# Block-turned probabilities placed by DMA, and a values product that runs one unit later

## The chip, the cores and the metric

One core of one Trainium2 chip runs the whole program. The metric is the device time of one execution in microseconds (us). TensorE is PE in the rows of the profile, VectorE DVE, ScalarE ACT, GpSimd POOL, and SyncE SP.

## What is computed

Eight batch elements of 128 rows and 512 columns go through three adapter layers (a base product plus a low-rank product, a product with a selected weight, a low-rank product, each added to its input), and then through an attention layer. There the kernel makes, per batch element and group of four query heads (8 key heads x 8 elements = 64 units):

```python
q = rope(rmsnorm(x @ Wq)); k = rope(rmsnorm(x @ Wk)); v = x @ Wv
k_all, v_all = concat(cached 512 rows, 128 new rows)      # 640 keys, heads of 128
scores = einsum('bqhd,bkhd->bhqk', q, k_all) * SCALE      # masked by cache length
out = softmax(scores) @ v_all, then @ Wo, added to x
```

All of it is f32 in and out. A product that has to be exact is made of three products of rounded parts: hi x hi, hi x lo and lo x hi, where hi is the operand rounded to fp32r and lo the rest.

## The kernel before

Instructions are written out by hand for each engine, in order, with semaphores between them; nothing reorders them. The adapter layers take the first 119 us. Then comes a loop over 64 units; unit n is batch element n & 7 of key head n >> 3.

TensorE's `step(n)` (L870) holds: scores of heads 0 and 1 (`score_pair`, L831, 12 products into three PSUM banks), eight of the twelve products of the next unit's queries (L800), scores of heads 2 and 3, the other four query products, the output product of the unit before (`put_out`, L848, 12 products of 512 columns), the transposes of chunks 0 and 1 of the probabilities (`turn_probs`, L856), the next unit's new key and value (`project_new_key`, L810), and then, chunk by chunk, four transposes of 128x128 and three products of 512 columns (`values`, L862). Among them lie the five transposes of the next unit's rotated queries and key (`turn_rotated`, L823) and the four of the cached keys of the unit after it (`turn_cached`, L816). Turned probabilities and turned keys go through two PSUM banks, `ps_ring`.

The probabilities are made in place: `lowest` (VectorE, L1110: scores from PSUM plus mask, with their minimum), `exps` (ScalarE, L620), `inverse` (VectorE, L1116), `normalize` (ScalarE, L625). Each turned chunk of 128 keys x 512 is evicted twice: rounded by ScalarE (`chunk_high`, L629, `pt_hi`), and its rest by VectorE (`chunk_low`, L1125, `pt_lo`). The values are split in the same way: `values_high` on VectorE (L1080), their rest on GpSimd (L476), the new value's parts on ScalarE and VectorE.

GpSimd (`step`, L468) also makes the rest of the weights, sums the rotated queries, takes the power for the norms (`norm_factors`, L464) and issues the two gathers of cached rows. SP (L331) issues the load of the next input `x_s` once `kv_proj` says that the last one is used, the load of a chunk of weights, and towards the end the stores of the output.

Names that the change and the prediction's steps touch: `kc_lo_out` counts the units whose cached keys are split, `qt_lo_out` those whose rotated queries are, `prob_done` the finished probability heads, `pv_done` the values products, `ot_lo_out` the split outputs, `vn_out` (new) the copies of the new value.

Of the kernel before, what the change touches and what calls it, by code (L numbers as in the profile page):

```python
# [31 lines left out]
AHEAD = B + 1  # L32
THETA = 10000.0
# [13 lines left out]
def build(nc, x, x_t, ids0, ids1, ids2, table, lens, w0_t, bias0, lora_a, lora_b, w1_t, w2_b, w2_a,  # L47
          w_qkvo, q_norm, k_norm, k_rows, v_rows, inv_freq, row_in_table, ident_in, out):
    ctx = ExitStack()
    with ctx:  # L50
# [142 lines left out]
        with ExitStack() as p2:  # L193

            rot_a = sb("rot_a", [P, GROUP + 1, D], scope=p2)
# [13 lines left out]
            v_hi = sb("v_hi", [P, CH, D], F32R, scope=p2)  # L209
            v_lo = sb("v_lo", [P, CH, D], F32R, scope=p2)  # L210
            prob = sb("prob", [P, GROUP, KEYS], scope=p2)
            pt_hi = sb("pt_hi", [P, CH, GROUP * P], F32R, scope=p2)
            pt_lo = sb("pt_lo", [P, CH, GROUP * P], F32R, scope=p2)
            ot_hi = sb("ot_hi", [P, GROUP * P], F32R, scope=p2)
            ot_lo = sb("ot_lo", [P, GROUP * P], F32R, scope=p2)
            mask = sb("mask", [P, KEYS], scope=p2)
# [5 lines left out]
            ps_ring = pb("ps_ring", [P, 2, 512], p2)  # L222
            ps_q = pb("ps_q", [P, 512], p2)
            ps_kv = pb("ps_kv", [P, 512], p2)
            ps_o = pb("ps_o", [P, 512], p2)
# [12 lines left out]
            v_hi_out, v_split, vn_hi_out, vn_lo_out = (psem(s) for s in ("v_round", "v_split", "vn_hi_out", "vn_lo_out"))  # L238
            scores, low_done, exp_done, inv_done, prob_done = (psem(s) for s in ("scores", "low_done", "exp_done", "inv_done", "prob_done"))
            p_turned, pt_hi_out, pt_lo_out = psem("p_turned"), psem("pt_hi_out"), psem("pt_lo_out")  # L240
# [9 lines left out]
            def keys_of(kt, u, lo, hi):  # L250

                return kt[:, bass.ds((u & 1) * KEYS + lo, hi - lo)]

# [3 lines left out]
            with nc.Block() as block:  # L257
                @block.sync
                def _(sp):
# [71 lines left out]
                    def step(n, weights, last, finished):  # L331
                        if not last:
                            sp.wait_ge(kv_proj, n + 1)
                            sp.nop(nofuse=True)
                            sp.dma_start(x_s[:, :, :].bitcast(F32), xt_dram[bass.ds((n + 1) & 7, 1), :, :, :].rearrange("a p s c -> p (a s) c")).then_inc(x_s_in, 16)
                        if weights:
                            sp.wait_ge(w_split, n + AHEAD)
                            sp.dma_start(w_raw[:, 0, :], w_qkvo[bass.ds(n + AHEAD, 1), :, :].rearrange("a p c -> p (a c)")).then_inc(w_raw_in, 16)
                        if finished:
                            sp.wait_ge(y_added, n)  # L340
                            sp.nop(nofuse=True)
                            sp.dma_start(out[bass.ds((n - 1) & 7, 1), :, :].rearrange("a p c -> p (a c)"),
                                         y[:, bass.ds((n - 1) & 7, 1), :].rearrange("p a c -> p (a c)")).then_inc(out_in, 16)
# [921 lines left out]
```

## Time and profile before

| | us |
|---|---|
| median of 3 runs | 1242.81 (1242.17 to 1243.01) |
| profiled execution | 1239.95 |
| its span, first to last instruction | 1238.1 |
| mean granted TensorE clock | 0.993 |

| engine | busy us | share of the span |
|---|---|---|
| PE matmul | 1212.0 | 98% |
| PE weight load | 1038.2 | 84% |
| DVE | 918.8 | 74% |
| ACT | 853.2 | 69% |
| POOL | 545.5 | 44% |

The difference between the span and the execution's time, 1.85 us, lies outside of the instructions. In a timeline row the first number is the start and the second the time from there to the end of the last instruction of the row, so that the start of the next row less that of this one is what the row costs its engine where nothing waits. Brackets at the end of a row give the idle time ahead of it and what ended it. DMA engines are busy for about a quarter of the time.

### The profile page before, as it was taken

How to read it: one execution, taken by the hardware profiler on the slowest of the kernel's cores; microseconds unless marked ns; L12 is line 12 of the kernel's file. 1: busy time of each engine (PE TensorE's matmuls, PEld its weight loads, DVE VectorE, ACT ScalarE, POOL GpSimd, SP SyncE). 2: the span in 40 equal slices, each digit the busy share in tenths (PEclk: the TensorE clock that was granted, in tenths of full speed). 3: DMA queues.
4: the chain of work that ended last, by engine and by line, in shares of the span. 5: the costliest groups of instructions: out<-in, count | busy, mean ns of one | idle time of the engine just before them, and what ended most of it. 6: DMA issues, size and time to landing. Idle time of an engine off the chain costs nothing.

```text
span 1238.1 us, 28992 instructions
## 1 busy us (share of the span) xinstructions
PE 1212.0 (98%) x7072; PEld 1038.2 (84%) x7072; DVE 918.8 (74%) x2295; ACT 853.2 (69%) x2170; POOL 545.5 (44%) x570
## 2 busy tenths in 40 slices
PE   7998999999999999999999999999999999999997
PEld 4565888888888888888888888888888888888885
DVE  2336778777778777787787877877778777777774
ACT  2233777777777777777777777777777777767774
POOL 7761444445444444444444444444544445333430
PEclk9998999999999999999999999999999999999999
DMA  6673222222222222222122222222222222112210
GB/s 193 232 255 107 78 67 78 89 89 67 75 80 89 89 62 80 80 89 89 61 74 87 89 86 65 72 89 89 78 67 77 89 89 69 63 59 85 85 52 25
DMA packets 37607, 109.50 MB, mean 88 GB/s; under 512 B 7512, under 2 KB 7640, under 8 KB 36570
## 3 DMA queue, kind: packets, MB, share of 16 engines
q1 hardware_dynamic: 25288, 68.44, 16.1%
q0 software_dynamic: 11152, 36.72, 10.4%
q10 hardware_dynamic: 1154, 4.19, 0.9%
q8 instruction: 6, 0.10, 0.0%
q14 instruction: 7, 0.06, 0.0%
HBM read 103.03 MB, written 6.29 MB: 88 GB/s over the span
## 4 chain that ended last, share of the span: by engine, by line
PE 96%; DVE 1%; ACT 1%; DMA 1%; issue 1%; POOL 0%; SPq 0%; DVEq 0%; ACTq 0%; POOLq 0%
PE ps_q L794 14%; PE ps_ring L858 12%; PE ps_o L694 11%; PE ps_o L696 11%; PE ps_o L695 11%; PE ps_kv L794 7%; PE ps_s L696 6%; PE ps_s L694 6%; PE ps_s L695 6%; PE ps_l L726 2%; PE ps_ring L820 2%; PE ps_q L828 2%; PE ps_t L688 1%; PE ps_l L742 1%; PE ps_h L712 1%
## 5 line engine op out<-in xcount | busy, mean ns | idle before, releaser
L622 ACT ACTIVATE prob<-prob,low 128x640 f32<-128x640 f32 x256 | 210.8, 824 | 129.0 <-DVE low L1112 128.9
L1028 DVE TENSOR_TENSOR pt_lo<-ps_ring,pt_hi 128x512 fp32r<-128x512 f32 x320 | 209.1, 686 | 87.8 <-ACT pt_hi L582 87.5
L1112 DVE CUSTOM_DVE_ANT_0 prob<-ps_s,mask,q_gain 128x640 f32<-128x640 f32 x256 | 216.3, 882 | 36.8 <-PE ps_s L696 35.0
L103 POOL TENSOR_TENSOR w_lo<-w_raw,w_hi 128x640 f32 (+1 forms) x64 | 100.2, 1565 | 263.6 <-DVE w_hi L97 262.3
L582 ACT ACTIVATE pt_hi<-ps_ring 128x512 fp32r<-128x512 f32 x320 | 181.5, 593 | 33.1 <-PE ps_ring L858 33.0
L627 ACT ACTIVATE prob<-prob,inv 128x640 f32<-128x640 f32 x256 | 196.9, 818 | 0.0
L858 PE MATMUL ps_ring<-ident,prob 128*128 128x128 f32 x1280 | 186.3, 276 | 5.1 <-DVE pt_lo L1028 2.7
L858 PEld LDWEIGHTS ps_ring<-ident,prob 128*128 128x128 f32 x1280 | 149.0, 141 | 40.3 <-DVE pt_lo L1028 9.9
L794 PE MATMUL ps_q<-w_hi,x_s 128*128 (+1 forms) x512 | 171.8, 396 | 0.0
L694 PE MATMUL ps_s<-kt_hi,qt_hi 128*128 (+1 forms) x512 | 159.4, 311 | 1.5 <-DVE low L1112 1.5
L696 PE MATMUL ps_s<-kt_hi,qt_lo 128*128 (+1 forms) x512 | 159.5, 311 | 0.0
L695 PE MATMUL ps_s<-kt_lo,qt_hi 128*128 (+1 forms) x512 | 159.1, 311 | 0.0
L476 POOL TENSOR_TENSOR v_lo<-v_raw,v_hi 128x512 fp32r<-128x512 f32 x64 | 83.4, 1302 | 154.6 <-DVE v_hi L1085 154.6
L694 PE MATMUL ps_o<-pt_hi,v_hi 128*128 128x512 f32 x320 | 147.6, 461 | 0.0
L696 PE MATMUL ps_o<-pt_hi,v_lo 128*128 128x512 f32 x320 | 126.9, 397 | 0.0
L695 PE MATMUL ps_o<-pt_lo,v_hi 128*128 128x512 f32 x320 | 125.6, 392 | 0.0
L466 POOL TENSOR_TENSOR rstd<-var,neg_half 128x5 f32<-128x5 f32 x64 | 77.4, 1209 | 85.9 <-DVE var L1061 85.8
L794 PEld LDWEIGHTS ps_q<-w_hi,x_s 128*128 128x128 f32 x512 | 95.6, 188 | 15.0
L794 PE MATMUL ps_kv<-w_hi,x_s 128*128 (+1 forms) x512 | 106.8, 293 | 0.0
L694 PEld LDWEIGHTS ps_s<-kt_hi,qt_hi 128*128 128x128 f32 x512 | 97.0, 189 | 7.5 <-DVE low L1112 1.8
L694 PE MATMUL ps_o<-w_hi,ot_hi 128*128 (+1 forms) x256 | 101.0, 394 | 1.4 <-DVE ot_lo L1028 1.4
L695 PEld LDWEIGHTS ps_s<-kt_lo,qt_hi 128*128 128x128 f32 x512 | 96.9, 189 | 5.7
(141 smaller groups left out, 2587.8 us busy)
## 6 DMA issues: line engine op xcount, KB each, us to landing
x_s<-xt_split SPq DMA_DIRECT2D x64, 512.0 KB, 3.3
w_raw<-w_qkvo_dram SPq DMA_DIRECT2D x55, 320.0 KB, 3.5
w<-w_t_dram SPq DMA_DIRECT2D x8, 1024.0 KB, 6.8
xt_split<-x3t ACTq DMA_DIRECT2D x8, 512.0 KB, 4.3
w_raw<-w_qkvo_dram POOLq DMA_DIRECT2D x9, 320.0 KB, 4.9
xbt<-x_t_dram SPq DMA_DIRECT2D x8, 256.0 KB, 2.9
xb<-x_dram SPq DMA_DIRECT2D x8, 256.0 KB, 3.7
out_dram<-y SPq DMA_DIRECT2D x8, 256.0 KB, 2.2
```

What stands on the lines that cost most here:

```text
L103: return nc.gpsimd.tensor_tensor(lo, raw, hi.bitcast(F32), ALU.subtract)
L476: nc.gpsimd.tensor_tensor(vl, v_raw[:, :], vh.bitcast(F32), ALU.subtract).then_inc(v_split, 1)
L582: return nc.scalar.activation(dst, src, ACT.Copy)
L622: nc.scalar.activation(prob[:, h, :], prob[:, h, :], ACT.Exp, bias=low[:, h:h + 1], scale=-1.0, accum_out=total[:, h:h + 1]).then_inc(exp_ ...
L627: nc.scalar.activation(prob[:, h, :], prob[:, h, :], ACT.Copy, scale=inv[:, h:h + 1]).then_inc(prob_done, 1)
L694: nc.tensor.matmul(dst, lh, rh, start=first, stop=False)
L695: nc.tensor.matmul(dst, lh, rl, start=False, stop=False)
L696: return nc.tensor.matmul(dst, ll, rh, start=False, stop=final)
L794: mm = nc.tensor.matmul(dst, x_s[:, int(i % 3 == 2), k * P:(k + 1) * P], w_rest if i % 3 == 1 else w, start=i == 0, stop=i == 3 * KT - 1)
L858: mm = nc.tensor.transpose(ps_ring[:, bank, h * P:(h + 1) * P], prob[:, h, c * P:(c + 1) * P], ident[:, :])
L1028: return nc.vector.tensor_tensor(dst, src, high.bitcast(F32), ALU.subtract)
L1112: nc.vector.tensor_tensor_reduce(out=prob[:, h, :], in0=ps_s[:, score_slot(h):score_slot(h) + KEYS], in1=mask[:, :], scale=q_gain[:, h:h + ...
```

## The change

- The probabilities are no longer transposed on TensorE and not split. VectorE transposes each head's 128x640 probabilities in blocks of 32x32 (`turn_blocks`) into `blocks`, and 16 DMAs (`place_block`), each of 32 partitions x 640 f32 (80 KB), put block rows where a full transpose has them, in one of two homes of `prob_t`. SP issues 12 of them, ScalarE 4, after the fourth head's transpose and after the values product of two units before.
- The values product takes `v_raw` and the new value as they are, in plain f32: ten products of 128x128 by 256 columns, in two halves (heads 0, 1 and heads 2, 3) with a PSUM bank each. It stands last in TensorE's `step(n + 1)`. Its second half uses the bank in which the next unit's cached keys have been turned, and waits for `kc_lo_out`.
- The output product and the addition to `y` are made one unit later still (`put_out(n - 2)` in step n).
- The query projection is in one piece between the score pairs. The new key's projection stands right behind the second score pair, the cached keys' transposes behind that, now for unit n + 1.
- ScalarE does the squares of unit n + 1 and the copy of its new value ahead of `exps(n, 2)`. VectorE's order is new as below. GpSimd moves the new value, and issues the gather of values at the start of its step.
- Two more steps are written out in front of the loops, and the end has `put_out` and `values` behind the last step.

```diff
+            def place_block(issuer, n, a, j):
+                issuer.dma_start(prob_t[j * BLOCK:(j + 1) * BLOCK, bass.ds((n & 1) * NB * RUN + a * RUN, RUN)],
+                                 blocks[a * BLOCK:(a + 1) * BLOCK, j, :, :, :].rearrange("p c h q -> p (c h q)")).then_inc(pt_in[j], 16)
...
+                    def place_blocks(n, first=False):      # SP; ScalarE's has a = 3 alone
+                        sp.wait_ge(blocks_turned, GROUP * (n + 1))
+                        if not first:
+                            sp.wait_ge(pv_done, 2 * (n - 1))
+                        for a in range(NB - 1):
+                            for j in range(NB):
+                                place_block(sp, n, a, j)
...
+                    def step(n, last, head=True, out=True, first=False):      # ScalarE
+                        if head:
+                            out_high(n - 2, 1, first=first)
                         exps(n, 0)
                         exps(n, 1)
                         normalize(n, 0)
                         normalize(n, 1)
+                        if not last:
+                            query_squares(n + 1, range(GROUP))
+                            key_squares(n + 1)
+                            new_value(n + 1, first=not out)
                         exps(n, 2)
                         exps(n, 3)
                         normalize(n, 2)
+                        if not last:
+                            scale_key(n + 1)
+                            cached_high(n + 1, ps_o1, first=not out)
                         normalize(n, 3)
                         if not last:
                             rotated_high(n + 1)
+                        if out:
+                            out_high(n - 1, 0, first=not head)
+                        place_blocks(n, first=not head)
...
+                    def values(u, cached, first=False):      # TensorE
+                        pe.wait_ge(v_in, 16 * (u + 1))
+                        pe.wait_ge(vn_moved, u + 1)
+                        for j in range(NB):
+                            pe.wait_ge(pt_in[j], 16 * NB * (u + 1))
+                        if not first:
+                            pe.wait_ge(ot_lo_out, 2 * u)
+                        for pair in (0, 1):
+                            if pair == 1:
+                                pe.wait_ge(kc_lo_out, cached)
+                            for c in range(CH):
+                                v = v_raw[:, c * D:(c + 1) * D] if c < CCH else v_new[:, :]
+                                mm = nc.tensor.matmul(ps_o[pair][:, 0:PAIR], v, turned_probs(u, c, pair),
+                                                      start=c == 0, stop=c == CH - 1)
+                            mm.then_inc(pv_done, 1)
...
+                    def step(n, last, out=True, pv=True, first=False):      # TensorE
                         score_pair(n, 0)
                         if not last:
                             project_queries(n + 1)
                         score_pair(n, 1)
                         if not last:
                             project_new_key(n + 1)
+                            turn_cached(n + 1, ps_o1, 2 * (n - 1) if out else None)
+                        if out:
+                            put_out(n - 2, first=first)
                         if not last:
                             turn_rotated(n + 1)
+                        if pv:
+                            values(n - 1, n + 1 if last else n + 2, first=not out)
...
                     def variances(u, first=False):      # VectorE
                         dve.wait_ge(sq_done, (GROUP + 1) * (u + 1))
+                        dve.wait_ge(vn_out, u + 1)
...
+                    def turn_blocks(n, h, first=False):
+                        dve.wait_ge(prob_done, GROUP * n + h + 1)
+                        if h == 0 and not first:
+                            for j in range(NB):
+                                dve.wait_ge(pt_in[j], 16 * NB * n)
+                        nc.vector.transpose(blocks[:, :, :, h, :].rearrange("p j c q -> p c j q"),
+                                            prob[:, h, :].rearrange("p (c j k) -> p c j k", c=CH, j=NB)).then_inc(blocks_turned, 1)
...
+                    def step(n, weights, last, head=True, out=True, first=False):      # VectorE
+                        if head:
+                            out_low(n - 2, 1)
                         lowest(n, 0)
                         lowest(n, 1)
                         if weights:
                             weights_high(n)
                         inverse(n, 0)
                         inverse(n, 1)
+                        if not last:
+                            rotate_queries(n + 1)
+                            rotate_queries_rest(n + 1)
                         lowest(n, 2)
                         lowest(n, 3)
+                        turn_blocks(n, 0, first)
                         if not last:
                             variances(n + 1)
                             rotate_key(n + 1)
+                        turn_blocks(n, 1)
+                        inverse(n, 2)
+                        inverse(n, 3)
+                        if head:
+                            add_out(n - 2)
+                        turn_blocks(n, 2)
                         if not last:
                             rotated_low(n + 1)
                             gains(n + 1)
+                        turn_blocks(n, 3)
+                        if not last:
+                            cached_low(n + 1, ps_o1)
+                        if out:
+                            out_low(n - 1, 0)
                         if not last:
                             dve.wait_ge(low_done, GROUP * (n + 1))
                             set_mask(n + 1)
```

## Rows read from the trace of the kernel before

**Rows 1.** Stretch table: length; busy PE, PEld, DVE, ACT, POOL; clock; DMA share; GB/s:

```profile
150.00:1195.00 1045.00, 1043.73 (x6290) 920.77 (x6289) 827.60 (x2108) 777.53 (x1996) 457.57 (x475) 1.00 0.25 79
```

**Rows 2.** Timeline of TensorE, first scores of step 1 and of step 63:

```profile
140.25 0.28 PE L694 MATMUL ps_s<-kt_hi,qt_hi 128*128 x1
...
1212.42 0.28 PE L694 MATMUL ps_s<-kt_hi,qt_hi 128*128 128x256 f32 x1
```

**Rows 3.** Timeline of TensorE in one unit; start, length, line, operation:

```profile
606.76 0.28 PE L694 MATMUL ps_s<-kt_hi,qt_hi 128*128 x1
...
608.53 0.39 PE L794 MATMUL ps_q<-w_hi,x_s 128*128 x1
...
613.11 0.40 PE L694 MATMUL ps_o<-w_hi,ot_hi 128*128 x1
...
615.87 1.03 PE L858 MATMUL ps_ring<-ident,prob 128*128 128x128 f32 x8
616.66 0.36 PE L794 MATMUL ps_kv<-w_hi,x_s 128*128 x1
...
618.21 0.66 PE L858 MATMUL ps_ring<-ident,prob 128*128 128x128 f32 x4
...
624.04 0.28 PE L694 MATMUL ps_s<-kt_hi,qt_hi 128*128 x1
```

**Rows 4.** Timeline of TensorE in the adapter layers, plain f32 products, two passes each:

```profile
19.84 1.05 PE L712 MATMUL ps_h<-xbt,a 128*16 128x128 f32 x8
20.81 3.70 PE L726 MATMUL ps_l<-w,x1t 128*128 128x512 f32 x8
```

**Rows 5.** Timeline of VectorE in the same unit:

```profile
601.48 0.17 DVE L1061 TENSOR_SCALAR var<-sq 128x5 f32<-128x5 f32 x1
...
602.41 0.68 DVE L1028 TENSOR_TENSOR pt_lo<-ps_ring,pt_hi 128x512 fp32r<-128x512 f32 x1
...
605.23 0.69 DVE L1028 TENSOR_TENSOR qt_lo<-ps_q,qt_hi 128x512 fp32r<-128x512 f32 x1
...
606.03 0.16 DVE L1078 TENSOR_SCALAR q_gain<-rstd 128x4 f32<-128x4 f32 x1
...
606.66 0.49 DVE L97 CAST w_hi<-w_raw 128x640 f32 x1
...
612.76 0.88 DVE L1112 CUSTOM_DVE_ANT_0 prob<-ps_s,mask,q_gain 128x640 f32<-128x640 f32 x1
```

**Rows 6.** Timeline of ScalarE in the same unit:

```profile
612.88 0.83 ACT L622 ACTIVATE prob<-prob,low 128x640 f32<-128x640 f32 x1 [0.30 <-DVE low L1112]
...
614.52 1.54 ACT L627 ACTIVATE prob<-prob,inv 128x640 f32<-128x640 f32 x2
```

**Rows 7.** SP's queue, a queue's total, and DMA issues with median us to landing:

```profile
1.28 1.84 SPq L298 DMA_DIRECT2D y<-w_t_dram  x4
...
55.08 0.68 SPq L294 DMA_DIRECT2D a<-w_a_dram  x1
...
q1 hardware_dynamic: 25288, 68.44, 16.1%
...
a<-lora_a_dram SPq DMA_DIRECT2D x8, 32.0 KB, 2.4
...
a<-w_a_dram SPq DMA_DIRECT2D x8, 32.0 KB, 5.5
```

**Rows 8.** Timeline of TensorE and stretch table (granted clock) around gaps:

```profile
130.51 1.24 PE L858 MATMUL ps_ring<-ident,prob 128*128 128x128 f32 x8 [2.10 <-ACT prob L627]
...
132.00:136.00 4.00, 4.00 (x23) 3.82 (x22) 2.45 (x8) 2.16 (x9) 1.11 (x2) 0.64 0.13 28
...
1215.85 0.39 PE L694 MATMUL ps_s<-kt_hi,qt_hi 128*128 128x256 f32 x1 [1.49 <-DVE low L1112]
...
1216.00:1220.00 4.00, 4.00 (x22) 3.60 (x23) 2.80 (x9) 3.93 (x9) 1.30 (x1) 1.00 0.01 4
...
1223.50 0.90 PE L858 MATMUL ps_ring<-ident,prob 128*128 128x128 f32 x4 [1.40 <-DVE pt_lo L1028]
```

More of the change, by code:

```diff
@@ L466, in norm_factors, with move_new_value, step @@
                         nc.gpsimd.tensor_tensor(rstd[:, :], var[:, :], neg_half[:, :], ALU.pow).then_inc(rstd_done, 1)
-                    def step(n, weights, keys, last):
-                        vl = v_lo[:, 0:CCH, :].rearrange("p c d -> p (c d)")
-                        vh = v_hi[:, 0:CCH, :].rearrange("p c d -> p (c d)")
+                    def move_new_value(u, values):
+                        pool.wait_ge(vn_out, u + 1)
+                        if values:
+                            pool.wait_ge(pv_done, 2 * u)
+                        pool.nop(nofuse=True)
+                        nc.gpsimd.tensor_copy(v_new[:, :], next_value(u)).then_inc(vn_moved, 1)
+                    def step(n, weights, keys, last, first=False, second=False):
+                        if not first:
+                            move_new_value(n - 1, not second)
+                            if not second:
+                                next_values(n - 1)
                         if weights:
@@ L487, in _ @@
                     next_keys(1)
-                    with pool.Fori(0, UNITS - AHEAD) as n:
+                    step(0, True, True, False, first=True)
+                    step(1, True, True, False, second=True)
+                    with pool.Fori(2, UNITS - AHEAD) as n:
                         step(n, True, True, False)
@@ L669, in _ @@
                     key_squares(0)
+                    new_value(0, first=True)
                     second_low_rank(B - 1)
-                    cached_high(0, first=True)
+                    cached_high(0, ps_x, first=True)
                     scale_key(0)
@@ L870, in step @@
-                    def step(n, keys, last, first=False):
-                        if first:
-                            pe.wait_ge(kc_lo_out, 1)
-                            turn_cached(1)
+                    def step(n, last, out=True, pv=True, first=False):
                         pe.wait_ge(qt_lo_out, n + 1)
@@ L930, in _ @@
                     turn(ps_t3, x3, t3_done)
-                    step(0, True, False, first=True)
-                    with pe.Fori(1, UNITS - 2) as n:
-                        step(n, True, False)
-                    step(UNITS - 2, False, False)
-                    step(UNITS - 1, False, True)
+                    step(0, False, out=False, pv=False)
+                    step(1, False, out=False)
+                    step(2, False, first=True)
+                    with pe.Fori(3, UNITS - 1) as n:
+                        step(n, False)
+                    step(UNITS - 1, True)
+                    put_out(UNITS - 2)
+                    values(UNITS - 1, UNITS)
                     put_out(UNITS - 1)
@@ L1188, in _ @@
                     set_mask(0)
-                    step(0, True, False, first=True)
-                    with dve.Fori(1, UNITS - AHEAD) as n:
+                    step(0, True, False, head=False, out=False, first=True)
+                    step(1, True, False, head=False)
+                    with dve.Fori(2, UNITS - AHEAD) as n:
                         step(n, True, False)
```

276 lines of the change are left out of this document (114 added, 162 removed).

## The prediction

> **What bounds the kernel now.** I read the stretch table first: over the steady stretch TensorE is busy in 1043.73 of 1045 us at full clock, VectorE in 828 and ScalarE in 778 [rows 1]. So the unit loop is TensorE's instruction stream without gaps, and the other engines fit under it. The reader is to see that a cut on VectorE or ScalarE is worth nothing here, and a cut on TensorE is worth its length only as long as nothing else ends last. The period comes from the TensorE timeline: step 1 starts its scores at 140.25 and step 63 at 1212.42, so 62 steps take 1072.17, 17.29 each [rows 2]. Inside one unit [rows 3], all as start-to-start differences: a score pair 1.77 (606.76 to 608.53); two pairs and the twelve query products 6.35 (to 613.11), so the queries 2.81; the output product 2.76; eight transposes 0.79, 0.099 each; the new key 1.55; and from 618.21 to 624.04 5.83 for 12 probability transposes, 15 value products and 9 other transposes.
>
> **TensorE's work, part by part.** Removed: 20 probability transposes and 15 value products of 512 columns. That is 0.79 + 5.83 less the 9 kept transposes (0.89) = 5.73 us per unit [rows 3]. Added: 10 value products in plain f32, 128x128 by 256 columns. A f32 product is two passes (the rows show x8 for four products). A pass takes 0.121 at 128 columns (0.97 between the starts of the two rows, over 8) and 0.46 at 512 (3.70 over 8) [rows 4]. No f32 pass of 256 columns is in the trace; between these rows it is 0.235, so 0.47 a product, 2.35 for each half of five, 4.7 in all (bounds: 0.21 and 0.27 a pass, 4.2 to 5.4). Dense, TensorE needs 17.29 - 5.73 + 4.7 = 16.25 us. If nothing else ended last, the gain would be 1.0 us per unit.
>
> **VectorE and ScalarE, sums.** VectorE loses five chunk subtractions, the rounding of the values and a small rest, and gains four block transposes of 128x640 f32. None is in the trace. Nearest: the reducing pass over 640 columns, 0.88 long; a 512-column two-input pass, 0.69; the 640-column cast, 0.49, which runs at a faster rate [rows 5]. Successive passes overlap by some 0.07. I take 0.75 (one pass over 640 columns at the ordinary rate), with ends 0.43 (the cast less the overlap) and 1.5 (twice the ordinary time). ScalarE loses five evictions and gains four DMA issues. Neither sum reaches 16 us, so it is order, not load, that decides.
> The Trainium skill (VectorE: DVE Perf Modes, The three transpose paths and Rules for kernel authors) speaks against the change: it sends a 128x128 transpose to TensorE if it may end in PSUM, and gives VectorE 311 ns for 128 columns of bf16. Five times that would be an estimate of 1.56 us here, the slow end again, and by it the time would be that of the slow rival below. The trace has no transpose on VectorE; its 640-column passes take 0.49 and 0.88, and so I stay with 0.75.
>
> **The walk through one unit of the changed kernel.** Time 0 is the start of scores pair 0 of step n.
> 1. TensorE: scores to 1.77, queries(n+1) to 4.58, scores pair 1 to 6.35, new key(n+1) to about 7.85, visible to others at 8.0 [rows 3]. Cached keys' transposes, then put_out(n-2) to 11.1.
> 2. ScalarE now has key_squares(n+1) and new_value(n+1) ahead of exps(n,2). Both need the new key, which TensorE now computes after scores pair 1. So exps(n,2), whose input is ready at 7.0, starts at 8.5 (estimates for two 128-column passes, 0.3 and 0.2), exps(n,3) ends at 10.2 (0.83 each [rows 6]).
> 3. VectorE: lowest(n,3) ends at 7.75 (scores of its pair done at about 6.1, two passes of 0.8), the first block transpose at 8.5; variances and the rotated key wait for new_value and take 0.93 (601.48 to 602.41 [rows 5]), to 9.5; the second block transpose to 10.25; only then the two inverses, 10.4. The wait added to variances holds those two, and through them normalize on ScalarE.
> 4. ScalarE: normalize(n,2) 0.77 (1.54 for two), scale_key 0.3 to 11.5, cached_high about 0.55 by its 512 columns, normalize(n,3) 0.77 to 12.85, rotated_high about 0.75 to 13.6 [rows 6]. key_scaled comes at 11.6, so turn_rotated, which TensorE reaches at 11.1, waits 0.5. It ends at 12.1, and the first half of the values runs to 14.5.
> 5. VectorE: add_out and the third block transpose end by 12.6 and wait for rotated_high; rotated_low 0.80 (605.23 to 606.03 [rows 5]) and gains to 14.5; the fourth block transpose to 15.25; cached_low (0.69) to 15.95.
> 6. TensorE's second half of the values goes into the bank that holds the turned keys of n+1, so it waits for cached_low: from 14.5 to 16.0, a stall of 1.5. It ends at 18.35, and the next step's scores, same queue, follow.
> The cycle closes on itself: period about 18.4 against 17.29, **1.1 us longer per unit**, although TensorE has 1 us less to do. The transposes count three times (first, second and fourth) once they are over 0.75; below that the first hides under the new key.
>
> **The moved DMAs.** SP issues 12 after the fourth block transpose (15.25), ScalarE 4. Four issues in a row took 1.84, 0.46 each, and DMAs of 32 KB landed in 2.4 [rows 7]. SP: 5.5 + 2.4, landed at 23.2. Bandwidth is no tighter: the SP queue's 25288 packets took 16.1% of 16 engines over 1238 us, 126 ns each, so 512 packets of 2560 B are 4.0 us on 16 engines. First user is not the value product but the next step's first block transpose, which waits until the single block buffer is empty: 18.4 + 7.75 = 26.1. Slack 3 us, cost nothing. Behind the transfers on SP's queue stand the next x_s and weight loads, wanted at 26.4 at the earliest: hidden. ScalarE's four issues end near 17.1; behind them stands out_high of the second half, not ready before 18.5: hidden. GpSimd: the value gather is issued by 3.5 instead of mid-unit, wanted at 12; its moved copy is short; the rstd result is there at 10.1, wanted at 11.2.
>
> **Sum.** Steps 1 to 62: 62 x 1.1 = +69. Ends: in step 0 the next scores start after cached_low, some 2 us earlier than before, but step 1 starts at the low clock, +1.8; the last step gets serial: blocks turned at about 10.5, placed at 18.5, five products twice, evictions, output product, 30 to 31 against 25.7 now (1212.42 to 1238.1 [rows 2]), +5. In all +73 to +74. The profiled execution took 1239.95 with a span of 1238.1 and would become 1313; the median of the runs is 2.86 above it, so the forecast is 1242.8 + 73 = **1316 us**. With the ends of the transpose: at 0.43 the second inverse waits for exps instead and the period is 17.7, +25 and +4 at the ends, 1272; at 1.5 it is 18.4 + 3 x 0.75 = 20.6, 1453. The value pass at its ends moves a half by 0.25 to 0.35: -16 to +22.
>
> **Rivals.**
> - *The clock (slower still).* Rows: after 2.10 us without work TensorE ran at the low level (granted clock 0.64 over 132 to 136, where 0.50 is 1.2 GHz); after 1.40 at 1223.5, shortly behind another gap, too (four transposes take 0.90, eight took 1.03 in the steady stretch); after 1.49 at 1215.85 it did not (granted 1.00 over 1216 to 1220) [rows 3, 8]. My stall of 1.5 sits between these. A clock of 0.64 over 4 us is 4 x 0.36 = 1.44 us of full-speed work lost. If every unit lost that: 62 x 1.44 = +89, 1405. Likelier a part of the units. The Trainium skill warns of it (TensorE: Matmul & The Clock Gate, A second HAM failure mode: psum-queue depth-cycling): short idles between groups of matmuls each iteration can make the clock swing. By that rule the time is up to 1405; the trace shows both outcomes at nearly this gap. 20%, mostly between 1340 and 1405.
> - *Slow transposes or late blocks.* Transpose at 1.5: 1453. Or issues and landing as long as their longer rows (12 x 0.68 + 5.5 = 13.7 from 15.25, so 2.8 late [rows 7]): the first block transpose, which has no slack, moves the whole chain, 21.2, some 1490. 10%.
> - *TensorE stays the bound (the other side, faster).* One mechanism: ScalarE's and VectorE's chain from new key to cached_low closes before the first half of the values ends. For it: every such chain is hidden now [rows 1], and TensorE does have 1.0 less. Against: the walk has it 1.5 + 0.5 too long, with in-order waits I can name. It decides from 1.1 us of shortening (equal to before) and pays fully from 2.1: 1242.8 - 62 x 1.04 + 5 = 1183. 12%.
> - *Nothing measurable*: the chain shortened by just 1.1: 1243. 3%.
>
> **Chances and range.** Forecast (1255 to 1340) 55%, clock 20%, slow transposes or late blocks 10%, faster 12%, same 3%. A measurement of this kernel can tell about 0.2%, 2.5 us, from no change. Leaving out the faster side and what is beyond 1400: **1255 to 1400**. Faster 0.12, same 0.03, slower 0.85.
>
> **What would show it.** Right: TensorE idle about 2 us a unit, before the values' second half with VectorE kt_lo as releaser and before turn_rotated with ScalarE's rot; TensorE's share near 88%; a period of 18.4; the block transpose near 0.75; exps(n,2) waiting behind the new key; no wait of the block transposes on DMA. Wrong: TensorE at 97% and a period near 16.3, or the first block transpose waiting for DMA, or a granted clock well under 1 in the steady stretch.

## The result and the profile after

The changed kernel takes 1307.08 us (median of 4 runs, 1303.15 to 1307.77) against 1242.49 for the kernel before beside it on the same chip: a ratio of 1.0519, interval 1.0491 to 1.0548. The profiled execution is 1307.04 with a span of 1305.3, 67.2 more than before. The forecast was 1316, with the mechanism that the walk gave.

The page, its busy shares and its chain by engine:

```profile
PE 1170.1 (90%) x6112; PEld 968.9 (74%) x6112; DVE 852.1 (65%) x2167; ACT 682.7 (52%) x1914; POOL 475.4 (36%) x570
...
PE 57%; DVE 20%; issue 10%; ACT 9%; DMA 1%; DVEq 1%; SPq 1%; ACTq 1%; POOL 0%; POOLq 0%
```

Every engine does less than before and the kernel is longer. The same stretch as in [rows 1]:

```profile
150.00:1195.00 1045.00, 951.06 (x5113) 808.80 (x5112) 729.68 (x1899) 588.49 (x1675) 377.53 (x456) 1.00 0.51 146
```

TensorE is busy in 951 of 1045 us where it was busy in 1043.73; the clock is full; the DMA share has doubled. The list of waits (engine, tile, line, releaser: us in total, times, longest; over the whole span) says where the 94 us of the stretch are:

```profile
PE ps_o L923 <- DVE kt_lo L1067: 60.5, 61, 1.2
PE ps_q L890 <- ACT rot L661: 42.5, 62, 3.3
```

One wait of each kind a unit. The timeline of TensorE in one unit, whose first scores start at 596.96; the last row is the next unit's first product:

```profile
608.84 0.63 PE L890 MATMUL ps_q<-ident,rot 128*128 128x128 f32 x4 [0.56 <-ACT rot L661]
...
609.61 1.99 PE L923 MATMUL ps_o<-prob_t,v_raw 128*128 x8
611.44 0.59 PE L923 MATMUL ps_o<-prob_t,v_new 128*128 x2
613.01 1.99 PE L923 MATMUL ps_o<-prob_t,v_raw 128*128 x8 [0.98 <-DVE kt_lo L1067]
614.84 0.59 PE L923 MATMUL ps_o<-prob_t,v_new 128*128 x2
615.08 0.47 PE L759 MATMUL ps_s<-kt_hi,qt_hi 128*128 x1
```

The unit takes 615.08 - 596.96 = 18.12 us (17.29 before). From the start of the first half to that of the second are 3.40 us; the second half itself takes 2.07, so the stall before it costs 1.33, of which the bracket shows 0.98. VectorE in the same unit:

```profile
604.98 0.84 DVE L1165 STREAM_TRANSPOSE blocks<-prob 128x640 f32<-128x640 f32 x1
605.74 0.17 DVE L1101 TENSOR_SCALAR var<-sq 128x5 f32<-128x5 f32 x1
...
606.66 0.84 DVE L1165 STREAM_TRANSPOSE blocks<-prob 128x640 f32<-128x640 f32 x1
607.42 0.18 DVE L1152 RECIPROCAL inv<-total 128x1 f32<-128x1 f32 x2
...
611.46 0.83 DVE L1165 STREAM_TRANSPOSE blocks<-prob 128x640 f32<-128x640 f32 x1
612.22 0.65 DVE L1067 TENSOR_TENSOR kt_lo<-ps_o,kt_hi 128x512 f32 x1
```

A block transpose is 0.84 long, and the next operation starts 0.76 behind its start. The last two rows are the pair that decides: the fourth transpose stands ahead of `cached_low`, for which TensorE's second half waits. ScalarE, and under it the two queues that issue:

```profile
605.11 0.28 ACT L643 ACTIVATE junk<-ps_kv 128x128 f32<-128x128 f32 x1 [0.40 <-PE ps_kv L859]
...
605.54 0.83 ACT L687 ACTIVATE prob<-prob,low 128x640 f32<-128x640 f32 x1
...
607.58 0.83 ACT L692 ACTIVATE prob<-prob,inv 128x640 f32<-128x640 f32 x1 [0.31 <-DVE inv L1152]
608.31 0.39 ACT L661 ACTIVATE rot<-key_sum,rstd 128x128 f32<-128x128 f32 x1
...
612.49 2.48 ACTq L264 DMA_DIRECT2D prob_t<-blocks  x4
```
```profile
612.70 7.91 SPq L264 DMA_DIRECT2D prob_t<-blocks  x12
```

ScalarE pays 0.62 an issue and SP 0.66.

### The profile page after: what moved, and what is told of

It reads as the page before. It is cut to its first block, busy times and chain, and to the rows that moved or that the text cites. A ratio compares the mean times of both kernels' runs of the same rounds, so it can differ in the third digit from the quotient of the medians.

```text
span 1305.3 us, 29650 instructions
## 1 busy us (share of the span) xinstructions
PE 1170.1 (90%) x6112; PEld 968.9 (74%) x6112; DVE 852.1 (65%) x2167; ACT 682.7 (52%) x1914; POOL 475.4 (36%) x570
## 3 DMA queue, kind: packets, MB, share of 16 engines
q0 software_dynamic: 11152, 36.72, 10.6%
## 4 chain that ended last, share of the span: by engine, by line
PE 57%; DVE 20%; issue 10%; ACT 9%; DMA 1%; DVEq 1%; SPq 1%; ACTq 1%; POOL 0%; POOLq 0%
PE ps_q L859 14%; PE ps_o L923 12%; DVE blocks L1165 10%; PE ps_kv L859 7%; PE ps_s L759 6%; PE ps_s L761 6%; PE ps_s L760 6%; DVE kt_lo L1067 4%; ACT kt_hi L640 4%; ACT prob L692 2%; PE ps_l L791 2%; ACT rot L661 2%; DVE rot_b L1110 2%; DVE key_sum L1113 1%; SPq L264 1%
## 5 line engine op out<-in xcount | busy, mean ns | idle before, releaser
L923 PE MATMUL ps_o<-prob_t,v_raw 128*128 (+1 forms) x1024 | 257.9, 395 | 64.9 <-DVE kt_lo L1067 60.5
L923 PEld LDWEIGHTS ps_o<-prob_t,v_raw 128*128 128x128 f32 x1024 | 186.9, 192 | 124.7 <-issue 101.8
L1146 DVE CUSTOM_DVE_ANT_0 prob<-ps_s,mask,q_gain 128x640 f32<-128x640 f32 x256 | 215.6, 878 | 37.1 <-PE ps_s L761 36.9
L1165 DVE STREAM_TRANSPOSE blocks<-prob 128x640 f32<-128x640 f32 x256 | 213.8, 836 | 2.5 <-ACT prob L692 1.7
L692 ACT ACTIVATE prob<-prob,inv 128x640 f32<-128x640 f32 x256 | 203.6, 819 | 21.3 <-DVE inv L1152 21.3
L759 PE MATMUL ps_s<-kt_hi,qt_hi 128*128 (+2 forms) x512 | 172.3, 337 | 6.2 <-issue 3.4
L522 POOL COPY v_new<-v_next 128x128 f32 (+1 forms) x64 | 18.3, 286 | 419.3 <-PE ps_o L923 410.9
L761 PE MATMUL ps_s<-kt_hi,qt_lo 128*128 (+2 forms) x512 | 160.7, 314 | 0.0
L760 PE MATMUL ps_s<-kt_lo,qt_hi 128*128 (+2 forms) x512 | 160.3, 313 | 0.0
L1067 DVE TENSOR_TENSOR ot_lo<-ps_o,ot_hi 128x256 fp32r<-128x256 f32 x128 | 53.2, 415 | 155.3 <-ACT ot_hi L640 155.3
L511 POOL TENSOR_TENSOR rot<-rot_a,rot_b 128x512 f32<-128x512 f32 x64 | 83.4, 1302 | 85.6 <-DVE rot_b L1093 85.6
L759 PE MATMUL ps_x<-w_hi,ot_hi 128*128 (+1 forms) x256 | 106.5, 416 | 2.5 <-DVE ot_lo L1067 2.5
L859 PE MATMUL ps_q<-w_lo,x_s 128*128 (+1 forms) x256 | 101.6, 397 | 0.0
```

Source lines behind the costliest of these rows:

```text
L692: nc.scalar.activation(prob[:, h, :], prob[:, h, :], ACT.Copy, scale=inv[:, h:h + 1]).then_inc(prob_done, 1)
L759: nc.tensor.matmul(dst, lh, rh, start=first, stop=False)
L760: nc.tensor.matmul(dst, lh, rl, start=False, stop=False)
L761: return nc.tensor.matmul(dst, ll, rh, start=False, stop=final)
L859: mm = nc.tensor.matmul(dst, x_s[:, int(i % 3 == 2), k * P:(k + 1) * P], w_rest if i % 3 == 1 else w, start=i == 0, stop=i == 3 * KT - 1)
L923: mm = nc.tensor.matmul(ps_o[pair][:, 0:PAIR], v, turned_probs(u, c, pair), start=c == 0, stop=c == CH - 1)
```

## The experiments

Twelve kernels, four batches; each ratio is to the kernel before in the same batch. First the walk's own links are undone one at a time.

**The key's subtraction ahead of the query's and of the fourth transpose** (VectorE):

```diff
                         if not last:
+                            cached_low(n + 1, ps_o1)
                             rotated_low(n + 1)
...
                         turn_blocks(n, 3)
-                        if not last:
-                            cached_low(n + 1, ps_o1)
```

> VectorE's cached_low(n+1) goes in front of rotated_low(n+1), where VectorE waits 0.63 us for ScalarE anyway; nothing else changes. Theory A (the closed chain new key - squares - exps - normalize - rotated_high - rotated_low - fourth block transpose - cached_low - second half of the values): the second half no longer waits (0.98 plus what surrounds it, 1.33 between the halves' starts less a half), so the chain closes at 16.8 instead of 18.11; but the block placement then comes due: the 12 issues on SP at 0.65 and a landing of 2.4 put the blocks 9.8 us behind the fourth transpose, and the next first transpose must wait for them, so the period is 16.9 to 17.0 and the time 1307 - 62 x 1.15 = 1236 (1228 to 1242). Rival B (TensorE's idle time is caused by the DMAs or by ScalarE's rotated key, not by this wait): 1300 or more. Rival C (only the length of the fourth transpose, 0.76, is won): 1260.

Measured: 1244.98 us, ratio 1.0024 (1.0003 to 1.0045). Moving one instruction gives back nearly all of the loss, and the second half's wait for `kt_lo` is gone from the list. So the wait named in the last step of the walk is the cause of most of the loss. The time expected was 9 us lower; the period is 17.13. One thing that takes over is ScalarE's queue of issues, in that kernel's timeline:

```profile
603.30 2.47 ACTq L264 DMA_DIRECT2D prob_t<-blocks  x4
606.19 0.39 ACT L640 ACTIVATE ot_hi<-ps_o 128x256 fp32r<-128x256 f32 x1 [2.96 <-issue]
```

The second half now ends sooner, and its eviction stands behind the four issues; in VectorE's order the eviction's rest precedes the next `lowest`. The walk had called these issues hidden, for a second half that ends 3.85 us behind the start of the fourth transpose; here it is 2.36 (the next scores start at 604.62).

The other is SP's placement, which the expectation had named. From a fourth block transpose to the first one of the next unit:

```profile
602.26 0.84 DVE L1165 STREAM_TRANSPOSE blocks<-prob 128x640 f32<-128x640 f32 x1
...
613.01 0.84 DVE L1165 STREAM_TRANSPOSE blocks<-prob 128x640 f32<-128x640 f32 x1
```

That is 10.75 us. The first issue comes 1.24 behind the fourth transpose, twelve take 7.9, and about 1.5 later the blocks are there (1.59 in the kernel with all issues on SP): 10.6. So in this kernel the two loops, through ScalarE's issues and through SP's, close within 0.2 us of each other, and it alone can't say which one holds.

**scale_key ahead of normalize(n,2)** (ScalarE):

```diff
                         exps(n, 3)
-                        normalize(n, 2)
                         if not last:
                             scale_key(n + 1)
+                        normalize(n, 2)
+                        if not last:
                             cached_high(n + 1, ps_o1, first=not out)
```

> ScalarE's scale_key(n+1) goes in front of normalize(n,2), into the 0.31 us in which ScalarE waits for the inverse. turn_rotated on TensorE then has its input about 1 us earlier and its wait of 0.6 us goes. Theory A: no change of the time (1307, within 3): turn_rotated is not on the chain, since rotated_high follows normalize(n,3) on ScalarE in any case; the idle time moves to the wait for cached_low, which grows from 0.98 to about 1.6. Rival (each idle gap of TensorE adds to the period): 62 x 0.6 = 37 us less, 1270.

Measured: 1287.93 us, 1.0345 (1.0310 to 1.0381), period 17.84. Neither number was met. The waits, in that kernel's list:

```profile
PE ps_o L924 <- DVE kt_lo L1068: 106.0, 62, 1.9
PE ps_q L891 <- ACT rot L661: 6.7, 4, 2.3
```

The wait before `turn_rotated` went, and the one at the second half grew (1.70 in a unit for 0.98), as two waits in series do. The period still fell by 0.28, which is about scale_key's own length (0.30 between 608.31 and 608.61 in the changed kernel): it stood between inverse and normalize(n,3) on the chain, and ahead of normalize(n,2) it fills the time in which ScalarE waited for the inverse (0.31). I had counted the order and forgotten the length of what was moved.

**Inverses ahead of the second block transpose** (VectorE):

```diff
-                        turn_blocks(n, 1)
                         inverse(n, 2)
                         inverse(n, 3)
+                        turn_blocks(n, 1)
```

> VectorE's inverse(n,2) and inverse(n,3) go in front of the second block transpose. Theory A: normalize(n,2) starts right behind exps(n,3), 0.3 to 0.4 us earlier, and everything behind it on the chain moves by that: period 17.75, 62 x 0.35 = 22 less, 1285 (1280 to 1290). Rival (VectorE's order here is covered, the chain is bound by the block DMAs or by the new key alone): 1307.

Measured: 1277.12 us, 1.0280 (1.0251 to 1.0310), period 17.71. That is 3 us under the expected range. normalize(n,2) follows exps(n,3) at once, without the 0.31 of waiting. So the second block transpose counts on the chain, by about 0.4 of its 0.76, until exps(n,3) is the later one.

**All sixteen DMAs on SP:**

```diff
-                        for a in range(NB - 1):
+                        for a in range(NB):
...
-                        place_blocks(n, first=not head)      # ScalarE
```

> All 16 block DMAs are issued by SP, none by ScalarE. Prices from the trace: 0.65 per issue, first issue 0.4 behind the fourth transpose, landing 2.4 behind the last issue. Theory A with the placement slack of 0.85 us per unit: 12 issues land 25.3 us after the start of the unit's scores against a need at 26.1; 16 land at 27.9, 1.75 late, which the first block transpose of the next unit waits for and which runs through the whole chain: period 19.8 to 19.9, 1307 + 62 x 1.75 = 1415 (1390 to 1425). Rival (the placement has several us of slack, as the prediction took it): 1307, or a little less because ScalarE is relieved. The clock may fall with the longer gaps, which would add to it.

Measured: 1412.51 us, 1.1361 (1.1333 to 1.1390). Its timeline closes a loop through the queue:

```profile
609.66 0.85 DVE L1164 STREAM_TRANSPOSE blocks<-prob 128x640 f32<-128x640 f32 x1 [1.57 <-DMA prob_t<-blocks]
...
629.37 0.85 DVE L1164 STREAM_TRANSPOSE blocks<-prob 128x640 f32<-128x640 f32 x1 [1.57 <-DMA prob_t<-blocks]
```
```profile
617.29 10.49 SPq L264 DMA_DIRECT2D prob_t<-blocks  x16
```

From the first block transpose to the first issue 7.63, sixteen issues 10.49, then 1.59 until the blocks are there: 19.71, the distance of the two rows. With twelve issues the same sum, counted on the changed kernel (7.72 from 604.98 to 612.70, 7.91, 1.6), is 17.2 against 18.12: a slack of about 0.9, not the 3 us of the prediction. TensorE waits about 2 us a unit in one piece here (2.13 in this unit, 2.14 in the median), and the mean granted clock falls to 0.942.

**ScalarE: exps(2) and (3) ahead of the key's square and the new value:**

```diff
                             query_squares(n + 1, range(GROUP))
-                            key_squares(n + 1)
-                            new_value(n + 1, first=not out)
                         exps(n, 2)
                         exps(n, 3)
+                        if not last:
+                            key_squares(n + 1)
+                            new_value(n + 1, first=not out)
                         normalize(n, 2)
```

> In the changed kernel, ScalarE does exps(n,2) and exps(n,3) ahead of the square and the copy of the new key instead of behind them. By the plain reading (the exps are held 0.8 us by the new key, so free them) it should gain, 62 x 0.8 = 50 us, 1257. Theory A: VectorE's variances wait for the copy of the new value, which now comes at 9.9 instead of 8.7, and behind that wait stand the second block transpose and the inverses that normalize needs: normalize(n,2) starts at 11.85 instead of 10.6, period 19.3, 1307 + 62 x 1.2 = 1381 (1365 to 1395).

Measured: 1394.16 us, 1.1191 (1.1163 to 1.1218), at the upper end of what the theory gave; the mean granted clock of 0.956 is in it. The plain reading of the walk's second step, that exps are late because the key's square stands ahead of them and that they should go first, gives 1257 and is wrong by 137 us: VectorE needs the squares for the norms before it reaches the inverses.

```profile
604.38 0.17 DVE L1102 TENSOR_SCALAR var<-sq 128x5 f32<-128x5 f32 x1 [1.04 <-ACT junk L643]
```
```profile
606.23 0.83 ACT L692 ACTIVATE prob<-prob,inv 128x640 f32<-128x640 f32 x1 [1.94 <-DVE inv L1153]
```
```profile
607.50 0.63 PE L891 MATMUL ps_q<-ident,rot 128*128 128x128 f32 x4 [1.69 <-ACT rot L661]
```

One wait on VectorE holds ScalarE 1.94 and TensorE 1.69. The order of the changed kernel is the better of these two, for all that it delays exps.

**Now the cures together.** The first two edits in one kernel:

> Both orders at once: cached_low in front of rotated_low on VectorE, scale_key in front of normalize(n,2) on ScalarE. Theory A (from the trace of the kernel with cached_low moved, period 17.13: the next bound is a loop through VectorE and ScalarE, first block transpose to fourth 7.2 us, then fourth to the next first 9.8 to 9.9, by way of the DMA issues on ScalarE ahead of out_high as well as by the placement on SP): scale_key's own 0.3 leaves the 7.2, the period becomes 16.8 to 16.9, 62 x 0.3 less than 1245: 1227 (1220 to 1234). Rival (TensorE's own work is what is left, 16.05 to 16.2): 1180 to 1190.

Measured: 1226.42 us, 0.9866 (0.9837 to 0.9895), within 1 us of the expectation and faster than the kernel before. The period is 16.91 and TensorE still waits 0.36 a unit for `rot`. Next, on top of both orders, ScalarE's issues behind the eviction of the second half, one step later:

```diff
                             out_high(n - 2, 1, first=first)
+                        if out:
+                            place_blocks(n - 1, first=first or not head)
                         exps(n, 0)
...
                             out_high(n - 1, 0, first=not head)
-                        place_blocks(n, first=not head)
```

> As the kernel with two orders moved, and ScalarE issues its four block DMAs one step later, behind out_high of the second half instead of in front of it. Theory A: out_high and the next unit's exps are no longer held by four issues of 0.62; then only the placement by SP is left at that place (last of 12 issues 7.6 us behind the fourth transpose, landing 2.1 to 2.4): period 16.6 to 16.9, 1213 to 1228. Rival (ScalarE's issues cost nothing): the same as the kernel with two orders. Rival (TensorE bound): 1180 to 1190.

> As the last, and the inverses of heads 2 and 3 in front of the second block transpose. Theory A: normalize(n,2) starts 0.07 earlier only, since scale_key now stands between it and exps: period 16.5 to 16.8, 1210 to 1225. If the chain through the second transpose were still binding by its full length, 0.4 per unit, 25 us less than the last.

Measured: 1229.28 (0.9888, 0.9860 to 0.9915), and with the inverses' order added 1231.25 (0.9888, 0.9863 to 0.9912). Nothing was gained: only the rival of no change is near. The lists of waits of the two kernels:

```profile
DVE blocks L1168 <- DMA prob_t<-blocks: 44.2, 62, 2.2
```
```profile
DVE blocks L1168 <- DMA prob_t<-blocks: 44.7, 62, 1.6
```

0.7 a unit, where it had been 2.9 us in all: the first block transpose now waits for the placement. It is SP's: ScalarE's four issues start 2.42 behind the fourth transpose and end by 4.9, SP's twelve end at 9.2. ScalarE's loop is open, exps(n,0) start 3.35 into the unit for 4.10, but the first block transpose still starts 10.77 behind the fourth one of the unit before. With the two orders alone it was 10.76, and there the last block that SP issued landed 10.60 behind. The second limit had been 0.15 us away. Whether the placements are all that is left was asked by leaving half of them out from the third unit on, with the counts of the waits to match; that half of the turned probabilities stays what the first units left there:

```diff
-                        for a in range(NB - 1):
+                        for a in range(NB - 1) if first else range(1):
```

> As the last, but from the third unit on only 8 of the 16 block DMAs are issued (4 by SP, 4 by ScalarE); the other half of the turned probabilities stays that of the first units, so part of the work is left out. Theory A: the placement then lands some 5 us earlier and leaves the loop; what is left is TensorE's own stream, 16.05 to 16.3, 1182 to 1198. Rival (the placement does not bind, but the order on VectorE and ScalarE does): no difference to the kernel that places all 16.

Measured: 1178.49 us, 0.9477 (0.9452 to 0.9501). Stretch from 150 to 1150, columns as in [rows 1]:

```profile
150.00:1150.00 1000.00, 995.33 (x5472) 871.48 (x5471) 783.65 (x2023) 628.25 (x1781) 394.81 (x481) 1.00 0.42 123
```

TensorE is the bound here, with a period of 16.2, and this is what the idea of the change is worth with placement at half its price: 5.2%. The last three kernels ask whether the full placement can be had without a longer period. GpSimd takes four issues of SP's, with a semaphore of its own (without and with the inverses' order):

```diff
-                        for a in range(NB - 1):      # SP
+                        for a in range(NB - 2):
...
+                        pool.wait_ge(blocks_turned, GROUP * (n + 1))
+                        if not (first or second):
+                            pool.wait_ge(pv_done, 2 * (n - 1))
+                        for j in range(NB):
+                            place_block(pool, n, NB - 2, j, pt_pool)
```

> As the kernel with ScalarE's issues behind out_high, and GpSimd, which is idle from 10.2 to 18 us of the unit, issues four of the blocks in place of SP, with a semaphore of their own. SP has 8 issues left: the last starts 2.6 us earlier, so the blocks land ahead of the next first transpose, if GpSimd's four (about 1 us each) land in about 2.5 to 3.4. Theory A (the placement by SP is the last bound): period 16.2 to 16.4, 1180 to 1195, and VectorE's block transposes no longer wait for the DMA. Rival (the DMA engines or their ports are full, not the issuing): no change, 1229.

> The same with the inverses in front of the second transpose too. Theory A: TensorE's stream is the bound in both, so no difference to the last (within 4 us).

Measured: 1221.77 (0.9807, 0.9785 to 0.9830) and 1219.40 (0.9790, 0.9769 to 0.9811). The second was within 4 us of the first as expected; both miss the time. SP's loop is open (waits of `blocks` on a DMA: 1.6 us in all), but ScalarE's issues stand ahead of exps(n,0), and they take longer. Timelines of the first of the two, ScalarE and VectorE:

```profile
613.97 2.93 ACTq L265 DMA_DIRECT2D prob_t<-blocks  x4
617.01 0.83 ACT L694 ACTIVATE prob<-prob,low 128x640 f32<-128x640 f32 x1 [3.03 <-DVE low L1157]
```
```profile
615.76 0.08 DVE L1157 DVE_READ_ACCUMULATOR2_ANT low<- 128x1 f32 x1
...
618.78 0.16 DVE L1163 RECIPROCAL inv<-total 128x1 f32<-128x1 f32 x1 [0.65 <-ACT prob L694]
619.15 0.69 DVE L1099 TENSOR_TENSOR rot_a<-ps_q,cos_q 128x512 f32<-128x512 f32 x1 [0.21 <-issue]
```

The row names `low` as the releaser of exps(n,0), but `low` was written at 615.84 and the exps started at 617.01, at the end of the issues: a releaser that had long been done. The four issues take 2.93 here. With half of the blocks left out they stand in the same place and take 2.5, exps(n,0) start 3.4 into the unit in place of 3.8, and TensorE is still the bound: the place alone does not cost the 0.6 of the period. The rest of this chain goes through GpSimd, whose rstd ScalarE's `rot` waits for by 0.55 a unit. So in the last kernel ScalarE issues nothing, SP eight and GpSimd eight (two values of `a` in the loop above in place of one):

> The kernel of the three orders with GpSimd issuing, but ScalarE issues nothing: SP issues 8 of the 16 DMAs and GpSimd 8 (the two of them at 0.54 to 0.65 us an issue). Theory (ScalarE's four issues, 2.93 us in front of exps(0), are the bound that is left): exps(0) starts as soon as lowest is done, about 1.2 us earlier; the stream of TensorE (16.2 us) then bounds or nearly so, period 16.2 to 16.5, 1185 to 1205 us. Rival (the placements: eight issues of GpSimd end later than four did, about 4.3 us behind the last block transpose, and the first block transpose of the next unit waits for them; or the DMA descriptors made by GpSimd slow its own work, the summed queries and the power for the norms): 1215 to 1235 us, with waits of VectorE's blocks on DMA or of ScalarE's rot on GpSimd's rstd in the list of waits.

Measured: 1220.31 us, 0.9800 (0.9777 to 0.9824): the rival. ScalarE's exps(n,0) start at once, and the chain runs through GpSimd, whose timeline from its issues to the norms has one wait, 0.80 for the row numbers of the gather:

```profile
613.00 4.36 POOL L265 DMA_DIRECT2D prob_t<-blocks  x8 [3.58 <-DVE blocks L1167]
617.50 0.29 POOL L523 COPY v_new<-v_next 128x128 f32 x1
617.76 0.18 POOL L493 COPY v_row<-row_id 128x1 int32 x1
618.74 1.01 POOL L496 DMA_INDIRECT v_raw<-v_rows_dram,v_row  x1 [0.80 <-POOL v_row L493]
619.77 1.60 POOL L105 TENSOR_TENSOR w_lo<-w_raw,w_hi 128x640 f32 x1
621.31 1.31 POOL L512 TENSOR_TENSOR rot<-rot_a,rot_b 128x512 f32<-128x512 f32 x1
622.74 1.20 POOL L516 TENSOR_TENSOR rstd<-var,neg_half 128x5 f32<-128x5 f32 x1
```
```profile
624.04 0.40 ACT L669 ACTIVATE rot<-key_sum,rstd 128x128 f32<-128x128 f32 x1 [0.50 <-POOL rstd L516]
```

A usual unit takes 16.6 here (the same issues start at 613.00 and at 629.57). The weights' rest, `w_lo`, is made only while there are weights to come, for the last time at 1041.6. Behind that, in the same kernel and with all sixteen DMAs in place:

```profile
1099.75 4.36 POOL L265 DMA_DIRECT2D prob_t<-blocks  x8 [3.71 <-DVE blocks L1167]
...
1106.70 1.30 POOL L512 TENSOR_TENSOR rot<-rot_a,rot_b 128x512 f32<-128x512 f32 x1
1108.84 1.20 POOL L516 TENSOR_TENSOR rstd<-var,neg_half 128x5 f32<-128x5 f32 x1 [0.84 <-DVE var L1102]
...
1115.81 4.36 POOL L265 DMA_DIRECT2D prob_t<-blocks  x8 [3.72 <-DVE blocks L1167]
```

The period is 16.06 there, GpSimd waits for its input again, and TensorE is the bound. So the full placement does fit under TensorE's own work where the weights' work is gone, 1.6 us a unit on GpSimd (and 0.5 for the cast on VectorE, which the chain of this kernel does not pass through). No run here moves the weights' rest to another engine. And once in twelve units one issue of GpSimd's starts 3.46 us behind the one before it, in place of 0.55; why is not shown:

```profile
346.80 0.50 POOL L265 DMA_DIRECT2D prob_t<-blocks  x1 [2.76 <-issue]
```

The five units with such an issue take 18.3 to 21.3, about 18 us of the whole time more than five usual ones.

So three ways to share out the sixteen issues (12 on SP and 4 on ScalarE; 8, 4 and 4; 8 on SP and 8 on GpSimd) end at ratios of 0.987, 0.981 and 0.980 and periods of 16.9 to 16.8 in the mean, while half of the issues is 16.2. The three with GpSimd's issues lie within each other's intervals: about 2% faster than the kernel before, 7% faster than the change as it was made.

## Why the prediction was right, step by step

Times from the start of the unit's first scores; the changed kernel's are rows above less 596.96.

| step of the walk | predicted | measured |
|---|---|---|
| exps(n,2) start, behind key square and new value | 8.5 | 8.58 |
| second block transpose starts (behind the norms' work) | 9.5 | 9.70 |
| inverses | 10.4 | 10.46 |
| scale_key starts | 11.2 | 11.35 |
| turn_rotated waits | 0.5 | 0.56 |
| fourth block transpose | 14.5 to 15.25 | 14.50 to 15.26 |
| stall before the second half | 1.5 | 1.33 |
| second half starts | 16.0 | 16.05 |
| second half ends, period | 18.35 | 18.12 |

- **The bound and the mechanism: right.** The two waits have the releasers that were named, and undoing the last link (1307 to 1245) and the inverses' link (to 1277) shows that both count. The walk along in-order queues gave each start in the table within 0.2 us, from rows of the kernel before alone. Two that don't hold the chain came later than it said: the first block transpose at 8.02 for 7.75, and the values' first half at 12.65 for 12.1. TensorE's share is 90% for the expected 88.
- **Block transpose, 0.75 taken, 0.76 measured.** The row it was set by, an ordinary pass over 640 columns, was the right neighbour. My estimate of 1.56 us, five times the 311 ns that the Trainium skill gives for 128 columns of bf16 (VectorE: DVE Perf Modes, The three transpose paths), did not hold here.
- **The term that was mis-sized: the values' half.** 2.35 predicted; 613.01 to 615.08 is 2.07, so 0.207 a pass, just under the lower bound of 0.21 that I gave. That is 0.28 a unit, and about the difference of the period (18.4 and 18.14): 61 x 0.26 = 16 us of forecast too much.
- **Dense TensorE: 16.25 predicted, 16.22 measured** in the kernel with half the placements, but by errors that cancel, which is luck. Its two halves take 4.22 for the 4.7 predicted (between the bounds of 4.2 and 5.4); the new key takes 1.42 for 1.55, too; the first score pair, the nine other transposes and the output product take 1.95, 1.13 and 2.91 where the rows of before gave 1.77, 0.89 and 2.76. Small groups of another kind of product in between cost at the joints: the first scores behind the f32 products take 0.30 to the next start (606.97 to 607.27), the others 0.12.
- **The placement: right that it costs nothing, wrong by how much.** An issue took 0.66, not the 0.46 of four issues from DRAM [rows 7], and the slack was 0.9 in place of 3. The bounds in the rival (0.68 an issue) held the value. It did not show in the time, yet the cures ran into it: the issues, on SP, ScalarE or GpSimd, are what kept the kernels with all sixteen DMAs from 1183, the time given to the rival with TensorE as the bound.
- **The last step: +5 predicted, +11.4 measured** (37.1 for 25.7; 1305.3 - 1268.21). Rows of the changed kernel:

```profile
1290.55 3.75 PE L923 MATMUL ps_o<-prob_t,v_raw 128*128 128x256 f32 x8 [3.20 <-DMA prob_t<-blocks]
```
```profile
1280.91 7.78 SPq L264 DMA_DIRECT2D prob_t<-blocks  x12
```

  The first issue comes 12.7 after the step's start for 10.5, twelve take 7.8 for 5.5, and the products run at the low clock (granted 0.50 over 1290 to 1294; 3.75 for eight passes, 1.99 in the steady stretch), behind a wait of 3.20 us.
- **The balance.** Period 61 x 0.845 = 51.6 (161.91 to 1268.21 is 18.14 a unit, before 17.29); the first two steps 0.5; the last step 11.4; the start of the loop 3.7 (123.20 for 119.49; in the other kernels it was 118.6 to 125.1 with the same work ahead of it, so I don't put this down to the change). Together the 67.2. Against the forecast: period -16, first two steps -0.4, last step +6.4, start +3.7, and -2.8 because the profiled execution was as long as the median this time: -9, the distance from 1316 to 1307. That the total is nearer than its terms is luck.
- **The clock: the rival did not come.** The granted clock is 1.00 over the steady stretch with gaps of 0.56 and 0.98 in every unit. It came in the experiments: with one gap of 2.14 a unit in the median (1.31 to 3.12) the mean clock was 0.942, with 1.69 in the median (1.67 to 2.26) it was 0.956. The Trainium skill (TensorE: Matmul & The Clock Gate, A second HAM failure mode: psum-queue depth-cycling) tells of a kernel whose clock swings between its two levels with short idles between groups of matmuls. Such swings, 1.00 and 0.50 in turns in the steady stretch, are seen in those two kernels, and not in the changed one with its shorter gaps.

The instructive miss was the slack of the issues after the first cure. For SP's I expected the blocks 9.8 us behind the fourth transpose, and it was 10.75 to the first transpose that needs them; ScalarE's four I left out, as hidden, though that had been worked out for a period of 18.4. At 17 such a slack can be up to 1.4 smaller.

## What to carry to other kernels

Work that is taken off a full engine pays only if every chain through the other, in-order queues closes within the new period: write down the start of each instruction along the chain, one column per engine, from rows of the trace, before the code. A DMA has a price of its own on the queue that issues it, here 0.55 to 0.73 us; sixteen a unit are about 10 us that stand in somebody's loop, so count issues as instructions and reckon their slack anew with each shorter period. When a stall goes, what was hidden by it shows up: look for the next latest link first (here the second one was 0.15 us away), and don't move an instruction ahead without the time of the instruction itself.

## What the runs showed of the hardware

- A 128x640 f32 transpose in blocks of 32x32 on VectorE: 836 ns, 0.76 from start to start; `lowest`, a pass over the same columns, is 878 ns.
- A DMA issue of 32 partitions x 640 f32 within SBUF, the length of a row over its number: 0.66 us on SP; 0.62 on ScalarE, and 0.73 while GpSimd issued too; 0.55 on GpSimd (4.36 for eight), with one issue in twelve units 3.46 behind the one before it. The blocks were usable 1.6 to 1.9 us after the last issue had ended (629.37 less 627.78 with all on SP; 1290.55 less 1288.69 in the last step).
- Plain f32 products of 256 columns: 0.207 us a pass in a dense row of ten, and the next product of another kind starts 0.2 late.
- Doubling the DMA share (0.25 to 0.51) lengthened no passing operation that I looked at: `lowest` is 0.88 in both kernels.
